# A fused cross-attention kernel on one core: first half of q formed on thirds of its inputs, v's weights loaded last, the last but one output products behind the last transposes

## The reference, cut to what matters

```python
text, ip = ctx[:, :-4], ctx[:, -4:]
q = heads(x @ W_q); k_t = heads(text @ W_k); v_t = heads(text @ W_v)
probs = softmax(einsum(q, k_t) * 16 ** -0.5)
text_out = probs @ v_t
k_ip = heads(ip @ W_k_ip); v_ip = heads(ip @ W_v_ip)
qsem = l2norm(einsum('bhst,bte->bhse', probs, text)); ip_n = l2norm(ip)
fused = einsum(q, k_ip) * 16 ** -0.5 + 0.5 * einsum(qsem, ip_n)
probs_ip = softmax(fused) * fside_S_0[None, None, :, None]
out = (text_out + probs_ip @ v_ip) @ W_out + b_out + x
```

## Time and profile before

| | us |
|---|---|
| median of 3 runs | 393.39 |
| lowest, highest | 393.24, 395.64 |
| the profiled execution | 393.96 |
| its span (first to last instruction, with the last landing) | 391.5 |
| TensorE busy | 378.1 (97%) |
| VectorE, ScalarE, GpSimd busy | 221.3, 210.5, 209.0 |

### The profile page before, as it was taken

The page is one execution under the profiler, slowest core; times in us unless marked ns, Lnnn a source line. Parts: engine busy times, 40 slices in busy tenths (PEclk is TensorE's granted clock), DMA queues, the critical chain, the costliest instruction groups (busy, mean ns, idle before and its releaser), DMA issues.

```text
span 391.5 us, 9455 instructions
## 1 busy us (share of the span) xinstructions
PE 378.1 (97%) x3605; PEld 319.6 (82%) x3605; DVE 221.3 (57%) x491; ACT 210.5 (54%) x493; POOL 209.0 (53%) x231
## 2 busy tenths in 40 slices
PE   7999999999999999999999999999999999999984
PEld 5688898787889888888888898888888888887673
DVE  1699482766456646663466545663566557644434
ACT  2753235585556554656455554747454566558621
POOL 8001290574638652796258642776259424934962
PEclk9999999999999999999999999999999999999999
DMA  8879996264117420480228220661119010001010
GB/s 244 286 178 226 248 196 146 95 153 94 59 40 192 78 71 2 155 146 20 76 80 176 54 85 2 196 112 47 42 42 180 10 41 3 2 14 30 2 32 16
DMA packets 29329, 37.89 MB, mean 97 GB/s; under 512 B 14346, under 2 KB 26619, under 8 KB 28603
## 3 DMA queue, kind: packets, MB, share of 16 engines
q1 hardware_dynamic: 28388, 36.22, 38.5%
q10 hardware_dynamic: 896, 1.07, 0.9%
HBM read 28.36 MB, written 8.81 MB: 95 GB/s over the span
## 4 chain that ended last, share of the span: by engine, by line
PE 87%; DVE 4%; DMA 3%; ACT 2%; POOL 2%; issue 1%; SPq 0%; ACTq 0%; DVEq 0%; POOLq 0%
PE PR L1024 41%; PE Y L1024 27%; PE P L1024 9%; PE O L1024 8%; DVE mx L912 2%; DMA pb<-wq 1%; DMA qst<-ma 1%; PE PR L1203 1%; ACT big L763 1%; POOL t L627 1%; POOL pb L600 1%; PE PR L1140 1%; DVE pb L935 0%; ACT er L767 0%; SPq L493 0%
## 5 line engine op out<-in xcount | busy, mean ns | idle before, releaser
L600 POOL TENSOR_TENSOR pb<-pb 128x448 f32<-128x448 f32 x78 | 89.0, 1141 | 99.0 <-DVE pb L935 93.2
L912 DVE TENSOR_REDUCE mx<-PR 112x1 f32<-112x371 f32 x160 | 82.1, 537 | 74.0 <-PE PR L1024 73.7
L1024 PE MATMUL Y<-er,Gh 128*128 128x448 f32 x240 | 95.2, 397 | 2.3 <-ACT er L767 1.3
L935 DVE TENSOR_TENSOR pb<-big,Y 128x448 f32<-128x448 f32 x120 | 72.5, 620 | 35.5 <-PE Y L1024 35.3
L1024 PE MATMUL Y<-er,Gl 128*128 128x448 f32 x240 | 87.2, 363 | 0.0
L763 ACT ACTIVATE big<-P 128x448 f32<-128x448 f32 x120 | 65.1, 542 | 22.9 <-PE P L1024 22.6
L767 ACT ACTIVATE er<-big 128x448 fp32r<-128x448 f32 x120 | 69.3, 578 | 3.8
L1024 PEld LDWEIGHTS Y<-er,Gh 128*128 128x128 f32 x240 | 45.2, 188 | 13.7 <-DVE pb L935 9.0
L1024 PE MATMUL PR<-kst,qst 96*112 96x371 bf16 x160 | 50.6, 328 | 0.4 <-ACT Vt L755 0.2
L1024 PEld LDWEIGHTS Y<-er,Gl 128*128 128x128 f32 x240 | 45.2, 188 | 2.2
L1024 PE MATMUL P<-qst,kst 99*128 99x112 bf16 x480 | 41.9, 213 | 0.8 <-DMA qst<-ma 0.6
(11 more groups left out here) (195 smaller groups left out, 674.1 us busy)
## 6 DMA issues: line engine op xcount, KB each, us to landing
et<-ctxT SPq DMA_DIRECT2D x8, 752.0 KB, 4.3
kst<-kd SPq DMA_DIRECT2D x7, 720.0 KB, 7.1
kd<-ks SPq DMA_DIRECT2D x16, 288.0 KB, 2.9
qst<-qd SPq DMA_DIRECT2D x48, 70.0 KB, 2.5
kst<-kd SPq DMA_DIRECT2D x7, 480.0 KB, 9.4
kst<-kd SPq DMA_DIRECT2D x9, 240.0 KB, 8.9
qd<-kst SPq DMA_DIRECT2D x4, 336.0 KB, 6.2
vx<-xr SPq DMA_DIRECT2D x8, 140.0 KB, 2.7
```

The source lines that it names most:

```text
L600: pool.tensor_tensor(total, total, (pz, pm)[j], ALU.add).then_inc(s_S, 1)
L912: dve.tensor_reduce(mx[b % 2][:, h:h + 1], bank[0:S, 0:T], AX.X, ALU.max).then_inc(s_free[seq[u] % NR], 1)
L935: dve.tensor_tensor((pz, pm, pa[g % 2])[j], eb[g % 3][:, 448 * j:448 * j + 448], Y[y % 2][:, 0:448], ALU.mult).then_inc(s_P, 1)
L1024: return pe.matmul(o, st, mv, start=start, stop=stop, **kw)
```

## The change

Six edits; the rest of the kernel is as it was.

1. Three semaphores `s_xc[i]`, one for each third of x's first half with the same third of W_q. TensorE forms all three chunks of the first half of q with the third as the outer loop, in three banks, and waits for each third alone. WARM goes from 15 to 10.
2. v's weights are loaded on SyncE's queue behind x's second half, ahead of the side loads.
3. In round 4 of every batch from 1 to 6, S0 stands ahead of cT.
4. In `LAST`, round 0, S2 stands ahead of g0; the unit r(6, 0, 2) is held by `behind` until behind the next gram unit on VectorE.
5. In `LAST`, round 4, pw' and r0' stand ahead of cT, and o(6) is taken out. It stands behind cT(7) at the end, ahead of both parts of ot, its VectorE sum (unit "sum") behind "end" 2; the second part of vWo goes ahead of cT(7).
6. For that, cT(7) and cT0 write to tiles of their own (`cEh`, `cEl`, in the free `eh[0]`, `el[0]`), the last product is summed in Y[1], and the load of x's rows of batch 7 is issued ahead of the store of batch 6.

```diff
-WARM = 15
+WARM = 10
@@ ROUNDS, LATE, LAST
-          "p E g2 g1 pT g0 cT S0 S1 v o S2")
+          "p E g2 g1 pT g0 S0 cT S1 v o S2")
-LATE = "p g2 g1 pT g0 cT S0 S1 v S2 o"
-LAST = ("S0 v g2 S1 g1 g0 S2 T0 T1",
+LATE = "p g2 g1 pT g0 S0 cT S1 v S2 o"
+LAST = ("S0 v g2 S1 g1 S2 g0 T0 T1",
         "S0 r0 g2 S1 g1 g0 pw S2 v",
         "S0 r1 g2 S1 g1 r2 g0 S2 v",
         "S0 z g2 p S1 g1 g0 S2 v pT T0'",
-        "g2 cT r0' pw' g1 o g0 r1' v vW r2'")
+        "g2 pw' r0' cT g1 g0 r1' v vW r2'")
@@ master_schedule
     order += [("pv", NG * B - 1), ("z", b, 0), ("T", b, 1), ("p", b, 0), ("end", 0), ("cT0", b), ("vWo", b, 0), ("pw", b, 1)]
-    order += [("cT", b), ("ot", b, 0), ("vWo", b, 1), ("ot", b, 1), ("end", 1), ("z", b, 1), ("end", 2)]
-    order += [("pT", b), ("o", b)]
+    order += [("vWo", b, 1), ("cT", b), ("o", b - 1), ("ot", b, 0), ("ot", b, 1), ("end", 1), ("z", b, 1), ("end", 2)]
+    order += [("sum", b - 1), ("pT", b), ("o", b)]
@@ behind
-        if u[0] in ("K", "G", "GV") and u[1] >= 2 and u != ("K", 2, 0):
+        if u[0] in ("K", "G", "GV") and u[1] >= 2 and u != ("K", 2, 0) or u == ("r", B - 2, 0, 2):
@@ SyncE
-                                 xT[128 * c:128 * c + CW[c], 448 * n:448 * n + 448]).then_inc(s_x[n], 16)
+                                 xT[128 * c:128 * c + CW[c], 448 * n:448 * n + 448]).then_inc(s_x1 if n else s_xc[c], 16)
...
             load_x(1)
+            sp.dma_start(wv_s, wv.rearrange("(c p) n -> p c n", p=128)).then_inc(s_wr_, 16)
...
                 if u[0] == "o":
                     b = u[1]
+                    if b == B - 2:
+                        sp.wait_ge(s_out[(b + 1) % 2], 16 * ((b + 1) // 2))
+                        sp.dma_start(xs[(b + 1) % 2], xr[b + 1]).then_inc(s_xr[(b + 1) % 2], 16)
                     sp.wait_ge(s_fin, b + 1)
                     sp.dma_start(out[b], xs[b % 2]).then_inc(s_out[b % 2], 16)
-                    if 2 <= b + 1 < B:
+                    if 2 <= b + 1 < B - 1:
@@ ScalarE
-                act.dma_start(wq_s[0:CW[c], c, :], wq[128 * c:128 * c + CW[c], :]).then_inc(s_x[0], 16)
-            act.dma_start(wv_s, wv.rearrange("(c p) n -> p c n", p=128)).then_inc(s_wr_, 16)
+                act.dma_start(wq_s[0:CW[c], c, :], wq[128 * c:128 * c + CW[c], :]).then_inc(s_xc[c], 16)
...
                 elif u == ("wq",):
-                    act.wait_ge(s_x[0], 96)
+                    for c in range(3):
+                        act.wait_ge(s_xc[c], 32)
@@ VectorE
-                elif k == "o":
+                elif k == "sum" or k == "o" and u[1] != B - 2:
...
+                    rr, n = xs[b % 2], seq[("o", b)]
+                    src = PR[n % NR] if b < B - 1 else Y[1]
+                    dve.tensor_tensor(rr, src[0:S, 0:C], rr, ALU.add).then_inc(s_free[n % NR], 1)
@@ TensorE
+                    if u == ("q", 0, 0):
+                        for i in range(3):
+                            pe.wait_ge(s_xc[i], 32)
+                            if i == 2:
+                                pe.wait_ge(s_set, QFILLS)
+                            for c in range(3):
+                                last = mm(pro[c][0:CW[c], 0:448], wq_s[:, i, 128 * c:128 * c + CW[c]], xT_s[:, i, 0:448],
+                                          i == 0, i == 2)
+                                if i == 2:
+                                    last.then_inc(s_pp, 1)
+                        continue
+                    if k == "q" and u[2] == 0:
+                        continue
...
                     if part == 0:
-                        freed(pe, n - NR)
+                        pe.wait_ge(s_P, 3 * NG * B)
                         pe.wait_ge(s_cd, 1)
...
-                        mm(PR[n % NR][0:S, 0:C], cTh[:, c, :], woh[:, c, :], c == 0, False)
+                        mm(Y[1][0:S, 0:C], cEh[:, c, :], woh[:, c, :], c == 0, False)
```

More of the change, by code:

```diff
@@ L247, in build @@
         vrWo = et[0:H * NIP, 1, 0:C]
+        cEh, cEl = [w[:, 2, 0:3 * S].rearrange("p (c s) -> p c s", c=3) for w in (eh[0], el[0])]
         wq_s = pb[:, 0:960].rearrange("p (c n) -> p c n", c=3)
@@ L273, in build @@
         pro = [P[0][:, :], P[1][:, :], Y[0][:, :], Y[1][:, :]]
-        s_x = [sem(f"s_x{n}") for n in range(2)]
+        s_xc = [sem(f"s_xc{i}") for i in range(3)]
+        s_x1 = sem("s_x1")
         s_wi = sem("s_wi")
@@ L675, in _ @@
                 elif u == ("xq",):
-                    act.wait_ge(s_x[1], 48)
+                    act.wait_ge(s_x1, 48)
                     act.activation(xqh[:, 0:2, :], xT_s[:, 0:2, 448:896], ACT.Copy)
@@ L803, in _ @@
                     act.wait_ge(s_cp, 1)
-                    act.activation(cTh[:, 0, :], Y[0][:, 0:S], ACT.Copy).then_inc(s_ca, 1)
+                    act.activation(cEh[:, 0, :], Y[0][:, 0:S], ACT.Copy).then_inc(s_ca, 1)
                 elif k == "cT" and u[1] == B - 1:
                     filled(act, u)
-                    act.activation(cTh[:, 1:3, :], bank[:, S:3 * S].rearrange("p (c s) -> p c s", c=2), ACT.Copy).then_inc(s_cTh, 1)
+                    act.activation(cEh[:, 1:3, :], bank[:, S:3 * S].rearrange("p (c s) -> p c s", c=2), ACT.Copy).then_inc(s_cTh, 1)
                 elif k == "cT":
@@ L997, in _ @@
                     dve.wait_ge(s_cTh, b + 1)
-                    c = 0 if b < B - 1 else 1
-                    dve.tensor_tensor(cTl[:, c:3, :], bank[:, c * S:3 * S].rearrange("p (c s) -> p c s", c=3 - c),
-                                      cTh[:, c:3, :].bitcast(f32), ALU.subtract).then_inc(s_free[seq[u] % NR], 1)
+                    c, hi, lo = (0, cTh, cTl) if b < B - 1 else (1, cEh, cEl)
+                    dve.tensor_tensor(lo[:, c:3, :], bank[:, c * S:3 * S].rearrange("p (c s) -> p c s", c=3 - c),
+                                      hi[:, c:3, :].bitcast(f32), ALU.subtract).then_inc(s_free[seq[u] % NR], 1)
                 elif k == "cT0":
                     dve.wait_ge(s_ca, 1)
-                    dve.tensor_tensor(cTl[:, 0, :], Y[0][:, 0:S], cTh[:, 0, :].bitcast(f32), ALU.subtract).then_inc(s_cd, 1)
+                    dve.tensor_tensor(cEl[:, 0, :], Y[0][:, 0:S], cEh[:, 0, :].bitcast(f32), ALU.subtract).then_inc(s_cd, 1)
                 elif k == "vW":
@@ L1049, in _ @@
                             sl = slice(128 * c, 128 * c + CW[c])
[L1050 to L1055, removed]
+                            mm(d[0:CW[c], 0:448], wqh[:, i, sl], xqh[:, i, :], i == 0, False)
+                            mm(d[0:CW[c], 0:448], wqh[:, i, sl], xql[:, i, :], False, False)
+                            last = mm(d[0:CW[c], 0:448], wql[:, i, sl], xqh[:, i, :], False, i == 2)
                     elif k == "kip":
@@ L1249, in _ @@
                     b, part = u[1], u[2]
-                    n = seq[("o", b)]
                     if part == 0:
-                        freed(pe, n - NR)
+                        pe.wait_ge(s_P, 3 * NG * B)
                         pe.wait_ge(s_cd, 1)
@@ L1256, in _ @@
                     for c in ((0,), (1, 2))[part]:
-                        mm(PR[n % NR][0:S, 0:C], cTh[:, c, :], woh[:, c, :], c == 0, False)
-                        mm(PR[n % NR][0:S, 0:C], cTh[:, c, :], wol[:, c, :], False, False)
-                        mm(PR[n % NR][0:S, 0:C], cTl[:, c, :], woh[:, c, :], False, False)
+                        mm(Y[1][0:S, 0:C], cEh[:, c, :], woh[:, c, :], c == 0, False)
+                        mm(Y[1][0:S, 0:C], cEh[:, c, :], wol[:, c, :], False, False)
+                        mm(Y[1][0:S, 0:C], cEl[:, c, :], woh[:, c, :], False, False)
                 elif k == "o" and u[1] == B - 1:
@@ L1263, in _ @@
                     freed(pe, seq[("pT", b)])
-                    mm(bank[0:S, 0:C], pTs[:, :], vrWo, False, True).then_inc(s_ring, 1)
+                    mm(Y[1][0:S, 0:C], pTs[:, :], vrWo, False, True).then_inc(s_ring, 1)
                 elif k == "o":
```

9 lines of the change are left out of this document (2 added, 7 removed).

## The result

The changed kernel takes 389.87 us (median of 6 runs, 389.37 to 391.85), the kernel before, run beside it, 394.15 us (median of 6, 393.24 to 395.64). The ratio is 0.9887, with a 95% interval from 0.9861 to 0.9913: 1.1% faster, 4.5 us by the ratio, where 4.6 us were forecast. The forecast of 388.9 us was counted from a median of 393.39; the median of all six runs of the kernel before lies 0.8 us above that. The profiled execution took 390.13 us with a span of 387.7, against 393.96 and 391.5: 3.8 us.

A forecast was written before the change was run, and what follows sets the result against it. TensorE's order of work was taken to bound the steady part, leaving gains at the two ends: start 1.6, edit 3 0.4, edit 4 0.7, edit 5 1.9, together 4.6 us. Forecast 388.9 us, range 387.7 to 390.9.

The forecast's parts named there:

- the three signs by which the prediction called itself wrong: Wrong if K(0) starts above 14, pT waits for o(6), or weight loads in q take 331 ns.
- Start: 1.6 us forecast: Kernel's start: K(0) at 13.0 and the first score tile 1.6 us earlier, with 0.5 us either way for transfers.
- The context lands earlier: Start: with 0.66 MB of v's weights no longer ahead, the context lands 1.6 us earlier, near 11.1; bounds zero and 2.1.
- q ends at 12.2: Start: q's first half runs by thirds from 5.0, 2.4 us each, ending at 12.2 where it ended at 14.60.
- rival C: Start: q's matmuls run at the lower clock if the first third lands after 5.0; 1.8 us slower, 395.2; chance 0.04.
- passed the first part's gain on unchanged to the first score tile: From K(0) to the first score tile: later steps shift as a whole, so 1.6 us counts there too.
- Rival A: Start: the context does not land earlier, K(0) stays at 14.6, 3.0 us are left: 390.4; chance 0.2.
- Edit 3: 0.4 us forecast: Beginning of batch 6: S0's exp and copy move into cT's shadow, so TensorE's 0.42 us stall goes: 0.4 us.
- Edit 4: 0.7 us forecast: Batch 7 up to gram(39): TensorE's stalls of 0.58 and 0.68 us together give 0.7 us, bounds 0.3 and 1.0.
- the product goes at once and this stall goes: Batch 7: with r2 held on VectorE, g0(37)'s product no longer waits and g1(38)'s 0.68 us stall on TensorE goes.
- Edit 5: 1.9 us forecast: Batch 7's round 4: without o(6), g0(39) starts 1.9 us earlier; o(6) just fits at the end; net 1.85 us.
- Rival B: The end: pT waits for o(6) and ot, or cast and store cost; up to 1.5 us go: 390.4; chance 0.18.

The follow-up runs named there:

- all_but_o_moved: The changed kernel with o(6) back in its old place in round 4, against the changed kernel; 392.32 us, ratio 0.9932 to the kernel before.
- z_and_s2: Changed kernel with batch 7's z behind S1 in round 3 and S2 ahead of g0 in rounds 1 and 2 too; 390.45 us, ratio 0.9867.
- after_again: The changed kernel profiled a second time with no edit; one run, 390.25 us.
- before_thirds: The kernel before with only q's first half by thirds and ten warming matmuls, v's weights left on ScalarE's queue; 394.87 us, ratio 1.0021.

## Why the prediction was right, and where its steps were not

The total (4.6 us forecast, 4.5 by the ratio) held; three of its four terms did not have their size. That it came out so close is in part luck: the misses of 0.6 and 0.3 us in the start and edit 4 stand against 0.5 us in edit 3. Two of the three signs by which the prediction called itself wrong, K(0) above 14 and slow weight loads in q, came up in the first profile.

**Start: 1.6 us forecast, about 1.0 found.** The mean of the three profiles at the first S0 is 1.92 us for the changed kernel and 0.73 us for the one before, so 1.2; over the ten profiles with edit 2 it is 1.63, so 0.9. I take 1.0, with three profiles of the kernel before that differ by 2.0 us behind it; the median spans with edit 2 alone and with both edits say 1.1. "The context lands earlier" was right in kind and too small: the cast began at 12.69, 12.30 and 11.39 in the kernel before, and at 9.87, 10.39 and 9.89 in the changed one, 2.1 us between the means, where I took 1.6 from the pace of 0.41 MB per us; the bound at the slower pace was the better one. The step that failed is "q ends at 12.2": it took the weight loads' change at 4.6 us in one profile as belonging to the kernel. It varies from 4.6 us to past 7.3, and q's matmuls at the lower level take twice as long (0.75 us from load to load against 0.37); its thirds cost 2.6 us and not 2.4 at the higher one too; in four of the profiles with thirds and ten warming matmuls (the changed kernel's first two, all_but_o_moved, z_and_s2) K(0) came at 13.8 to 14.2 behind q. So part of rival C came true, the one named behind it, a few of q's matmuls at the lower level in some runs; it came without the late third that C made its condition. It did not make the kernel slower, since q starts 2 us earlier than it did. The other failed step is the one that passed the first part's gain on unchanged to the first score tile: the k tiles' load stands between, as inferred above, and it added 0.9 us in the first profile (K(0) 0.62, S0 1.52) and took up to 0.7 us in others.

**Rival A** (the context does not land earlier) is dead: the context landed 2.1 us earlier on the mean. At K(0) each edit leaves the other bound, as forecast: with edit 1 alone it waits 0.81 us for `el`, with edit 2 alone it comes behind q. In the time it is otherwise. Edit 2 alone gains (0.9963), edit 1 alone does not (1.0021, with the clock's fall in it), and the pair has the median span of edit 2 alone. That q's thirds are worth anything in the time is not shown; what they gain at K(0) the wait for the bias rows can take back.

**Edit 3: 0.4 us forecast, 0.8 found, plus 0.12 from gram(34) to gram(35).** The mechanism was right; the term was mis-sized because I took the 0.42 us shown as idle. The record before it (0.48 us long, 314.62) is drawn 0.3 us past the place at which gram(30) starts when nothing is waited for, 0.19 us behind it in after_again, and the idle time counts from its end; that makes 0.7 of the 0.8. From starts it is 8.18 - 7.37. That S0 in its new place could itself wait for a transfer, as in one profile, I had not named.

**Edit 4: 0.7 us forecast, 0.4 found.** S2 ahead of g0 gave 0.4 (gram(35) to gram(36): 1.63 to 2.03, and as much without the hold), near the 0.3 forecast for it. The hold gave nothing where I gave it 0.4. The step "the product goes at once and this stall goes" was right, and the stall did go; what is late next is ScalarE. It has z in its order ahead of the exp of S1, z waits for GpSimd's L664, whose chain begins with the power, and OT comes two exps and two copies later (367.93 to 370.19). I named GpSimd's chain as a bound for pT and missed that it holds ScalarE's order too.

**Edit 5: 1.9 us forecast, 1.88 to 1.90 found** from gram(39) to the last pT, in all six profiles with it and round 3 unchanged. Round 4 loses the wait and the nine matmuls, and the place at the end is free: pT still waits for `pe_`, by 0.39 us. The cast of vWo ended at 380.23 and cTh started at 380.20, as allowed for. Rival B is dead.

**The sum**, with these: 1.0 + 0.9 + 0.4 + 1.9 = 4.2 us, within the interval's 3.4 to 5.5.

The row of the kernel before that misled was right for its execution. What one profile can't tell is how much of it is the execution's own: here the first 65 us of one kernel vary by 2 us, and the part behind gram(30) by 0.1.

## What to carry to other kernels

Where a start is bounded by two inputs that end together, test each edit alone and both together before either gets a share: here one gave all that the times show. Take a second profile before a start is priced, since the moment of the clock's rise is no property of the code, and where a kernel loses time with no wait to show for it, look at the granted clock in the windows. Price a stall by the starts of the matmuls around it, not by the idle time shown in brackets. Before an instruction is freed from one engine's order, walk every other engine's order for the same chain: the stall that goes on TensorE may be there a second time on ScalarE.

## What the runs showed of the hardware that I had not expected

TensorE's higher level (loads of 187 to 190 ns in place of 330 to 340) came at 4.6 us in the first profile of the kernel before, and in three profiles of the changed kernel between 5.1 and 5.7, between 6.5 and 6.9, and after 7.26 us, with matmuls in unbroken order from 1.53 us in all of them and the granted clock shown as 1.00 throughout.
By the Trainium skill, "TensorE: Matmul & The Clock Gate", section "Part 1: The HAM clock gate", the point of the change varies between runs of one kernel, by about half a microsecond either way in its example; the traces agree that it varies, and show more, 2.6 us between the earliest and the latest.
The granted clock also fell in the middle of the kernel, to 0.52 and 0.62 in two stretches of 2 us (before_thirds, 66 to 70 us), at an engine that had idled 1.36 us and taken up its work again 1.2 us before the fall; the steps behind it came 1.4 us later.

Taking one 0.66 MB load from the other queue brought the context forward by 2.1 us (means of three profiles each, which spread over 1.3 us in the kernel before), more than the 1.6 us that its bytes take at the pace of 0.41 MB per us shown in the earlier trace rows. And TensorE waited up to 1.4 us for transfers of 4.4 KB behind a load of 1.4 MB in the same queue where they were issued 4.9 to 6.1 us after it, and not where they were issued 6.4 to 7.0 us after it.
